# Expert results scattered to token order by GpSimd during the group stage, in groups of 256 rows

## The reference

```python
scores = jax.nn.sigmoid(xt @ gate_w.T)
_, idx = lax.top_k(scores + gate_b, TOPK)            # TOPK = 4, 16 experts
w = take(scores, idx); w = w / sum(w) * ROUTE_SCALE
comb = zeros((T, 16)).at[arange(T)[:, None], idx].add(w)
y = sum over e of comb[:, e] * (silu(xt @ gate_e.T) * (xt @ up_e.T)) @ w2_e.T
y = y + the shared expert
x = x + tanh(g_ffn[0]) * y
```

## Time and profile before

| what | value |
| --- | --- |
| median of 3 runs | 1525.03 us (1523.73 to 1525.3) |
| span of the profiled execution | 1543.6 us, 1.2% above the median |
| PE busy | 1113.8 us, 72% |
| DVE busy | 1014.9 us, 66% |
| ACT busy | 637.1 us, 41% |
| POOL busy | 486.5 us, 32% |
| DMA | 146.24 MB, mean 95 GB/s |

### The profile page before, as it was taken

How to read it: one execution, slowest core, us unless ns; L and a number is a source line. 1 busy time by engine, 2 the same in 40 slices (tenths; PEclk the granted TensorE clock), 3 DMA queues, 4 the chain that set the end, 5 groups by cost and what they waited for, 6 DMA issues and landing times. The chain is left out here.

```text
span 1543.6 us, 23798 instructions
## 1 busy us (share of the span) xinstructions
PE 1113.8 (72%) x8155; PEld 569.9 (37%) x8155; DVE 1014.9 (66%) x1856; ACT 637.1 (41%) x1280; POOL 486.5 (32%) x539
## 2 busy tenths in 40 slices
PE   3799985342407999805465568999999999998757
PEld 2355553121204666502232323333333333331646
DVE  4899985455453766525556387888888888870665
ACT  0455553111102333201122207777677767775430
POOL 1243341767760000078777061111111111111110
PEclk7999997656657999956767759999999999995988
DMA  6001100222259999943656431111211121100003
GB/s 204 22 21 42 41 1 14 89 85 86 91 200 214 250 258 259 244 122 89 210 182 196 143 101 40 55 38 39 59 54 38 39 59 53 38 2 1 1 0 109
DMA packets 183649, 146.24 MB, mean 95 GB/s; under 512 B 102638, under 2 KB 160494, under 8 KB 183546
## 3 DMA queue, kind: packets, MB, share of 16 engines
q1 hardware_dynamic: 162570, 102.61, 25.3%
q0 software_dynamic: 12288, 33.57, 6.7%
q10 hardware_dynamic: 8688, 8.66, 1.7%
HBM read 53.11 MB, written 68.55 MB: 79 GB/s over the span
## 5 line engine op out<-in xcount | busy, mean ns | idle before, releaser
L1782 DVE TENSOR_REDUCE small<-ps 128x2 f32<-128x960 f32 (+6 forms) x384 | 379.0, 1040 | 56.8 <-PE ps L1837 56.5
L1761 ACT ACTIVATE region<-ps 128x512 f32<-128x512 f32 (+5 forms) x768 | 343.1, 532 | 110.0 <-PE ps L1851 108.6
L1732 POOL TENSOR_SCALAR_AFFINE_SELECT region<-region 128x512 f32<-128x512 f32 (+2 forms) x160 | 87.7, 548 | 427.4 <-ACT region L1761 427.4
L1851 PE MATMUL ps<-region 50*128 50x512 f16 (+5 forms) x896 | 198.6, 332 | 26.7 <-ACT region L1761 23.7
L1927 PE MATMUL ps<-region 128*32 128x512 f32 (+5 forms) x1792 | 192.9, 504 | 2.0 <-POOL region L1732 1.5
L1200 PE MATMUL ps<-region 128*128 128x384 f16 x696 | 125.2, 331 | 38.8 <-DMA region<-expert_rows 38.0
L859 POOL DMA_INDIRECT expert_rows<-region,small x128 | 130.6, 1020 | 65.1 <-issue 36.6
L1837 PE MATMUL ps<-region 48*128 48x480 f16 (+6 forms) x896 | 141.4, 333 | 13.5 <-DVE small L1782 11.3
L1365 POOL DMA_INDIRECT region<-result_rows,home x128 | 133.5, 1043 | 38.0 <-issue 36.8
L1851 PEld LDWEIGHTS ps<-region 50*128 50x128 f16 (+1 forms) x896 | 54.2, 95 | 211.3 <-ACT region L1761 195.6
L1200 PEld LDWEIGHTS ps<-region 128*128 x696 | 67.6, 99 | 83.5 <-issue 45.5
(11 more groups left out here) (237 smaller groups left out, 1693.3 us busy)
## 6 DMA issues: line engine op xcount, KB each, us to landing
result_rows<-region SPq DMA_DIRECT2D x58, 384.0 KB, 4.1
region<-v_parts SPq DMA_DIRECT2D x16, 576.0 KB, 4.1
v_parts<-region SPq DMA_DIRECT2D x14, 576.0 KB
region<-k_parts SPq DMA_DIRECT2D x96, 68.0 KB, 2.2
region<-q_parts SPq DMA_DIRECT2D x96, 64.0 KB, 2.1
k_parts<-region SPq DMA_DIRECT2D x16, 272.0 KB
x_sb<-in_x ACTq DMA_DIRECT2D x8, 512.0 KB, 9.1
region<-in_w13T SPq DMA_DIRECT2D x16, 256.0 KB, 3.0
```

The source lines that it names most:

```text
L1732: nc.gpsimd.affine_select(out=t, in_=t, compare_op=ALU.is_ge, fill=0.0, base=r0, pattern=[[0, G], [1, w]], channel_multiplier=-1).then_inc ...
L1761: nc.scalar.activation(dst, src, ACT.Exp, scale=SCALE).then_inc(s_exp, 1)
L1782: nc.vector.tensor_reduce(nmp[:, qt, :, p0:p0 + np_, place], s_pair(n + first)[:, :, 0:np_ * nk] .rearrange("p e (h k) -> p e h k", h=np_) ...
L1851: ins = nc.tensor.matmul(o, k_of(rr, tbuf)[:, pair, kt * P:kt * P + rows], q_of(rr, tbuf)[:, pair, q0:q0 + nq], start=True, stop=True)
```

## The change

A token copy now carries its destination. Each row of `expert_rows` grows from 256 to ROW = 272 numbers: 16 integers follow the data, and number e says in which row of `result_rows` the result of expert e for this token is to stand (token * 4 + rank). `targets(c)`, three VectorE instructions before `slots(c)`, writes them. The rows of the tail fill carry numbers past the end (from TRASH on), which the indirect DMA leaves out by its bounds check. In the group stage SyncE fetches for each group, behind the transposing DMA, the column of 256 targets of the group's expert (a 4-byte number from each row) into `gidx`; GpSimd scatters the group's results by it with two indirect DMAs of 128 rows. `homes`, `home` and the gathers of the projection stage go away: `result_rows` is now in token order, and SyncE reads each half chunk with one plain DMA (`fetch`). GROUP is 256, so that GROUPS = (16384 + 16 * 255) // 256 = 79; a group's output fits one PSUM bank, of which two alternate.

```diff
-GROUP = 3 * P
+GROUP = 2 * P
+ROW = D + E
-Y_BUFS = 4
+Y_BUFS = 6
+I_BUFS = 8
-STORE_LAG = 6
...
-                for g in range(GROUPS + STORE_LAG):
-                    if g < GROUPS:
-                        if g >= G_BUFS:
-                            sp.wait_ge(s_ggu, g - G_BUFS + 1)
-                        sp.dma_start_transpose(xgT[:, g % G_BUFS].rearrange("p s k n -> p (s k) n"),
-                                               xs[bass.ds(start(g), GROUP), :].bitcast(F16)).then_inc(s_xg[g % G_BUFS], 16)
-                    done = g - STORE_LAG
-                    if done >= 0:
-                        sp.wait_ge(s_yout, done + 1)
-                        sp.dma_start(ys[done * GROUP:(done + 1) * GROUP, :].rearrange("(j p) n -> p j n", p=P),
-                                     y_out[:, done % Y_BUFS]).then_inc(s_back[done % Y_BUFS], 16)
+                for g in range(GROUPS):
+                    if g >= G_BUFS:
+                        sp.wait_ge(s_ggu, g - G_BUFS + 1)
+                    first = start(g)
+                    sp.dma_start_transpose(xgT[:, g % G_BUFS].rearrange("p s k n -> p (s k) n"),
+                                           xs[bass.ds(first, GROUP), 0:D].bitcast(F16)).then_inc(s_xg[g % G_BUFS], 16)
+                    if g >= I_BUFS:
+                        old = g - I_BUFS
+                        sp.wait_ge(s_back[old % Y_BUFS], (old // Y_BUFS + 1) * GT * 16)
+                    e = sp.value_load(expert_tab[0:1, g:g + 1], min_val=1, max_val=E)
+                    sp.dma_start(gidx[:, g % I_BUFS, :],
+                                 xs[bass.ds(first, GROUP), bass.ds(e + (D - 1), 1)].bitcast(I32)
+                                 .rearrange("(j p) n -> p (j n)", p=P),
+                                 allow_slow_non_contiguous=True).then_inc(s_idx[g % I_BUFS], 16)
...
+                for g in range(GROUPS):
+                    pool.wait_ge(s_idx[g % I_BUFS], (g // I_BUFS + 1) * 16)
+                    pool.wait_ge(s_yout, g + 1)
+                    for j in range(GT):
+                        nc.gpsimd.indirect_dma_start(
+                            out=ys, out_offset=bass.IndirectOffsetOnAxis(ap=gidx[:, g % I_BUFS, j:j + 1], axis=0),
+                            in_=y_out[:, g % Y_BUFS, j, :], in_offset=None, bounds_check=B * L * TOPK - 1,
+                            oob_is_err=False).then_inc(s_back[g % Y_BUFS], 16)
...
+                def targets(c):
+                    pick(nc.vector.tensor_tensor(tagged[:], eq[:], nth[:].unsqueeze(1).unsqueeze(3)
+                                                 .to_broadcast([P, TC, TOPK, E]), ALU.mult))
+                    pick_order.wait()
+                    pick(nc.vector.tensor_reduce(tag[:], tagged[:].rearrange("p j r e -> p j e r"), AX.X, ALU.add))
+                    pick_order.wait()
+                    nc.vector.scalar_tensor_tensor(out=rows[:, c % ROW_BUFS, :, D:ROW].bitcast(I32), in0=tag[:],
+                                                   scalar=float(c * CH * TOPK),
+                                                   in1=token4[:].unsqueeze(2).to_broadcast([P, TC, E]),
+                                                   op0=ALU.add, op1=ALU.add)
...
+                def fetch(c):
+
+                    for t in range(TC // FETCH):
+                        sp.wait_ge(s_comb, c * TC * TOPK + 1 + (t + 1) * FETCH * TOPK)
+                        first = c * CH + t * FETCH * P
+                        sp.dma_start(yg[c % 2][:, t * FETCH:(t + 1) * FETCH].rearrange("p j r d -> p j (r d)"),
+                                     ys[first * TOPK:(first + FETCH * P) * TOPK, :]
+                                     .rearrange("(j p r) d -> p j (r d)", p=P, r=TOPK)).then_inc(s_yg[c % 2][t], 16)
...
+                for c in range(4):
+                    fetch(c)
+                for b in range(B):
+                    if 2 * b + 4 < 2 * B:
+                        fetch(2 * b + 4)
+                    store_parts(b)
+                    if 2 * b + 5 < 2 * B:
+                        fetch(2 * b + 5)
```

More of the change, by code:

```diff
@@ L144, in flamingo @@
     k_parts = nc.dram_tensor("k_parts", [B, KH, 2, PARTS, G * DH, KEYS], F16, kind="Internal").ap()
-    xs = nc.dram_tensor("expert_rows", [E * STRIDE + GROUP, D], F32, kind="Internal").ap()
-    ys = nc.dram_tensor("result_rows", [GROUPS * GROUP, D], F32, kind="Internal").ap()
+    xs = nc.dram_tensor("expert_rows", [E * STRIDE + GROUP, ROW], F32, kind="Internal").ap()
+    ys = nc.dram_tensor("result_rows", [TRASH + GROUP, D], F32, kind="Internal").ap()
     v_parts = nc.dram_tensor("v_parts", [UNITS, P, KT * G * 32], F32, kind="Internal").ap()
@@ L409, in flamingo @@
         iota_g = view(small, "iota_g", [P, GROUPS], F32)
+        nth = view(small, "nth", [P, TOPK], F32)
+        token4 = view(small, "token4", [P, TC], F32)
         tri = view(small, "tri", [P, P], BF16)
@@ L721, in flamingo @@
         reset(region0, region1, small)
-        rows = view(region0, "rows", [P, ROW_BUFS, TC, D], F32)
+        rows = view(region0, "rows", [P, ROW_BUFS, TC, ROW], F32)
         y_out = view(region0, "y_out", [P, Y_BUFS, GT, D], F32)
@@ L795, in flamingo @@
             s_back = [sem(f"back{i}") for i in range(Y_BUFS)]
+            s_idx = [sem(f"targets{i}") for i in range(I_BUFS)]
             block = sc.enter_context(nc.Block())
@@ L1067, in _ @@
                         statistics(c + 2)
+                    targets(c)
                     hidden(c)
@@ L1075, in _ @@
                         tables()
-                        for early in range(EARLY):
-                            homes(early)
                     add_shared(c)
@@ L1105, in _ @@
                         group_hidden_low(g + DEEP - 1)
-                    if g % 8 == 7 and EARLY + g // 8 < CHUNKS:
-                        homes(EARLY + g // 8)
             @block.tensor
@@ L1257, in flamingo @@
         junk = view(small, "junk", [P, 5], F32)
-        pause = view(small, "pause", [P, TC], F32)
         NBUF = 3
@@ L1334, in _, with store_parts @@
                     sp.dma_start(dst, src.rearrange("(k p) n -> p k n", p=P)).then_inc(s_in, 16)
-                for b in range(B):
+                def fetch(c):
[5 more added lines that the diff above has]
+                                     .rearrange("(j p r) d -> p j (r d)", p=P, r=TOPK)).then_inc(s_yg[c % 2][t], 16)
+                def store_parts(b):
                     sp.wait_ge(s_pstored, (b + 1) * P_STORES + 1)
@@ L1357, in _ @@
                 nc.gpsimd.memset(vs[:, :, :, DH:32], 1.0).then_inc(s_const, 1)
-                def fetch(c, t):
-                    pool.wait_ge(s_comb, c * TC * TOPK + 1 + (t + 1) * FETCH * TOPK)
-                    for j in range(t * FETCH, (t + 1) * FETCH):
-                        for r in range(TOPK):
-                            at_ = j * TOPK + r
-                            nc.gpsimd.indirect_dma_start(
-                                out=yg[c % 2][:, j, r, :], out_offset=None, in_=ys,
-                                in_offset=bass.IndirectOffsetOnAxis(ap=home[:, c, at_:at_ + 1], axis=0)
-                            ).then_inc(s_yg[c % 2][t], 16)
-                for c in range(2 * B):
-                    fetch(c, 0)
-                    if c:
-                        ln_pool(nc.gpsimd, c - 1, s_var, s_rstd)
-                    fetch(c, 1)
-                    if 1 <= c < 2 * B - 1:
-                        nc.gpsimd.tensor_tensor(pause[:], half[:], half[:], ALU.pow).then_inc(s_pause, 1)
-                        pool.wait_ge(s_pause, c)
+                for c in range(2 * B - 1):
+                    ln_pool(nc.gpsimd, c, s_var, s_rstd)
                 ln_pool(nc.gpsimd, 2 * B - 1, s_var, s_rstd)
```

55 lines of the change are left out of this document (23 added, 32 removed).

## The result

The changed kernel takes 1549.38 us (median of 4 runs, 1546.11 to 1554.11), the kernel before, on the same chip, 1524.38 (1517.62 to 1525.3): a ratio of 1.0163, 95% interval 1.0138 to 1.0187. It is slower by 25 us; the forecast was 1520.5.

A forecast was written before the change was run, and what follows sets the result against it. SyncE was to pace the group stage at 3.02 us a group (+67.8 us), GpSimd's gathers paced the projection stage and go (-72.4): -4.6 on the 1543.6 us span, 1520.5 us timed; range 1493 to 1560 us.

The forecast's parts named there:

- break-even at 3.08 us a group: Group stage: the step time at which the predicted loss and the projection stage's predicted gain sum to zero.
- SyncE dearer than read: Rival, group stage: transpose keeps 1.40 or fetch 0.59, a group takes 3.3 to 3.5 us, 1542 to 1558 us; 20%.
- Sum 0.71 + 1.12 + 0.71 + 0.40 + 0.08 = 3.02 us: Group stage, SyncE's issues per group: load, transpose of 256 rows, second load, target fetch, two gaps.
- Fills, -6.5 us: Before the first transpose: smaller fills and scatters, 6.69 MB instead of 8.39 at 260 GB/s, save 6.5 us.
- the row stage's +9: Row stage: `targets` adds 1.2 us a chunk ahead of `slots`, unhidden; eight chunks give 9.6, taken as +9.
- The timed runs stand at 0.988 of that span: Whole kernel: scaling from the profiled span of 1543.6 us to timed runs, giving 1525.03 - 4.5 = 1520.5 us.
- Tail of the group stage, 20.5 us: Group stage, behind the last transpose: landing, matmuls, copy, five GpSimd issues, last issue to reader and barrier, 20.5 us.
- Projection stage, 155 us: Projection stage without gathers: near 155 us long, chunks of 16.1 us, a gain of 72.4 us.
- 0.8 for `x_low` behind the stores: Projection stage: SyncE held by a pair's stores, some 2 us of `x_low` slip; chunk 16.1 instead of 15.3 us.
- 9.26 us for a chunk's products: Projection stage, one chunk: from TensorE's first product to the last `low`, 9.26 us of the chunk's 15.3.
- GpSimd's scatter was put at 1.33 with its gap: Group stage: GpSimd's two indirect DMAs at 1.33 us or less, 2.5 to 2.7 a group, below SyncE's 3.02.
- The rival of the strided transpose: Rival, group stage: rows 1088 bytes apart make transposes a third dearer, SyncE about 3.4 us a group, 1550 us; 7%.

The follow-up runs named there:

- groups_256_only: The kernel before with groups of 256 rows instead of 384 and nothing else of the change: 1554.79 us, ratio 1.0209 to the kernel before.
- plain_reads_only: The kernel before with plain reads of results replacing GpSimd's gathers in the projection stage, reordering left out: 1448.05 us, ratio 0.9490 to the kernel before.

## Why the prediction was wrong

The mechanism was seen: SyncE paces the group stage, and the projection stage loses its gathers and much of its length. The sign hung on a difference of two large terms, with break-even at 3.08 us a group. It was taken as 3.02; it is 3.34, and the rival "SyncE dearer than read" came true at 1549 us, inside its 1542 to 1558, though by other parts than it named: it wanted a transpose of 1.40 or a fetch of 0.59 (the second alone would have made 3.21, not the 3.3 that it gives). That the time lies there is in part chance, since two further errors all but cancel. From the typical trace of before the sum's terms miss by +6 us up to the first transpose, +26 in the group stage and -7 in the projection stage, 25 together.

*The step that failed: "Sum 0.71 + 1.12 + 0.71 + 0.40 + 0.08 = 3.02 us".* Measured means: transpose 1.27, gap with the second load 0.87, fetch 0.41, gap with the first load 0.80, together 3.35. The transpose was scaled with its rows from 1.40; 1.25 is what 256 rows cost, also with rows that lie without a gap (groups_256_only). That is 0.13 a group in the medians. The loads with their gaps are 1.57 in the median instead of 1.50: that the second also needs the address of a single column (register operations of 0.11 and 0.03 in the trace) was left out. The fetch was right. The last 0.14 are interruptions that an undisturbed step doesn't have, such as the transpose of 1.60 above. In the trace 40 of SyncE's instructions and gaps are over 0.1 us longer than their median, by 10.2 us in all or 0.13 a group: 26 are table loads, 8 are transposes and fetches, and 6 are gaps of 0.3 us that come every 38 to 40 us. The prediction added up quiet durations. What makes the interruptions is open. All of it is 78 x 0.32 = 25 us.

*Fills, -6.5 us.* It does not exist. The term was made from a trace in which the fills were late, for a reason that the traces do not show. Where they are not, GpSimd's last scatter sets the first transpose. Of the row stage's +9 the last scatter shows 463.20 - 454.84 = 8.4.

*The base.* "The timed runs stand at 0.988 of that span" was read as a harmless offset. It was the warning that the trace came from an untypical execution: a second one stands at 1524.1, as the timed runs do. The 20 us lay ahead of the first transpose (11), in the projection stage (6) and behind it (3), and the sum used the first two.

*Tail of the group stage, 20.5 us.* Measured 749.4 - 727.1 = 22.3.

*Projection stage, 155 us.* It is 141.8, and by plain_reads_only 145.0: 13 us better than forecast. The chunk was taken as 16.1, with 0.8 for `x_low` behind the stores; it takes 13.7 to 14.8 but for the first and the last, less than even the 15.3 without them. Part of that is TensorE's clock, 0.69 granted in the earlier trace rows and 0.80 after, which the sum had carried over in its 9.26 us for a chunk's products. In the last chunk the 36 products that took 7.99 us before, at a granted clock of 0.71, take 5.70 at 1.00:

```profile
874.28 5.70 PE L1537 MATMUL ps<-region 128*128 128x512 f16 x36 [2.10 <-DVE region L1476]
```

The gain from a typical trace of before is 79 us, not 72.

*Other engines.* GpSimd's scatter was put at 1.33 with its gap and is 1.28; the DMA engines stay at 0.69 in mid stage, and neither bounds the changed kernel. The rival of the strided transpose fell: its issue takes 1.25 us with rows 1088 bytes apart and with contiguous ones, and landing is 3.7 against 3.3 us in the median, far from a third more on SyncE. (The 2.02 us of the sixteen engines that the rival puts in mid stage are from the stage's first 9 us.) From 520 to 640 us a packet of 256 bytes took 22.4 ns of a DMA engine on average in the changed kernel and 21.6 in groups_256_only, and 18 in the median of both. The Trainium skill, page "DMA: Bandwidth & Descriptors", section "Latency and other measured facts", gives a lower rate for a transposing DMA whose middle dimension isn't contiguous; the landing times here go the same way, but TensorE waits here for transposes that are issued late, not for ones that land late, so that the runs don't test that rate.

Shown by experiment: that SyncE's issue time sets the step (a load added, loads joined, the fetch moved away), what each part costs, and that GpSimd, with the DMA engines beside it, is next. Only argued: how much of the projection stage's 13 us is TensorE's clock, and that the parts' costs add up.

## What to carry to other kernels

Count what a DMA-issuing engine does for each tile as carefully as what TensorE does: issue times, every load into a register (0.6 us here for one of its own with its check, 0.25 for a value in a joined one), every computed address (0.24 us, 0.41 with its check); none of it stands in a column of busy time, and little of it shrinks with the tile. Before a tile is made smaller, multiply the parts that don't shrink by the new count, and before two large terms are set against each other, compare the span of the trace with the timed runs: where it is over 1% off, find the stretch that is out of line first. When one engine's issues pace a stage, move an issue to an engine that waits anyway; here that turned a loss of 1.6% into a gain of 1.5%.

## What the runs showed of the hardware

- The issue of a transposing DMA shrinks little with its rows: 1.40 us for 384 rows of 1 KB when nothing is in front of it, 1.25 in the median for 256. A straight line through the two leaves 0.95 us without any row, which is an estimate.
- A register load on SyncE costs by the value: the instruction takes 0.27 us for one, 0.47 for two, 1.91 for eight. Alone, with its check and gaps, a load of one value lengthens the sequence by 0.61 us.
- An indirect scatter of 128 rows takes GpSimd 0.98 us for the result rows of 1024 bytes, and 0.96 in the row stage, with rows of 1024 bytes before and of 1088 after; in a row of them there are 0.30 us between two.
- The same program's eight fills took SyncE 12.4 us in one execution and 26.8 in another.
